# A condition layer's down products: five plain fp32 products against fifteen products of rounded pairs

## What is computed

```python
scores = softmax((x @ wt.T + repeat(g @ wg.T)) / 2)   # 8 experts, the best 2 kept, weights sum to 1
gp, up = leaky(x @ w_gate[e]), x @ w_up[e]            # 8 experts of 64 hidden columns
y = sum over the 2 chosen e of weight * (gp * up) @ w_down[e]
y = y + leaky(x @ sw_gate) * (x @ sw_up) @ sw_down    # shared expert, 128 hidden columns
```

## Time and profile before

| what | value |
|---|---|
| device time, median of 3 runs | 264.55 us (264.28 to 265.64) |
| the profiled execution's own time | 263.71 us |
| its span, first to last instruction | 261.9 us |
| TensorE busy | 246.4 us, 94% of the span |
| VectorE, ScalarE, GpSimd busy | 211.8, 147.5, 105.3 us |
| mean granted TensorE clock | 0.992 |
| share of the chain that ended last | PE 62%, DVE 17%, POOL 8%, ACT 5% |

### The profile page before, as it was taken

How to read it: one execution, slowest core, us unless ns; L and a number is a source line. 1 busy time by engine, 2 the same in 40 slices (tenths; PEclk the granted TensorE clock), 3 DMA queues, 4 the chain that set the end, 5 groups by cost and what they waited for, 6 DMA issues and landing times.

```text
span 261.9 us, 5119 instructions
## 1 busy us (share of the span) xinstructions
PE 246.4 (94%) x1848; PEld 196.8 (75%) x1848; DVE 211.8 (81%) x423; ACT 147.5 (56%) x239; POOL 105.3 (40%) x145
## 2 busy tenths in 40 slices
PE   7999999999999969988999999899999999999994
PEld 5877467667899849877687667677788888888884
DVE  7897868976876495889779987799998887888883
ACT  2666423445621454688455354687686677877550
POOL 3799310135581844864456758323220101101000
PEclk9999999999999998999999999999999999999999
DMA  6994510010210001211200000015290000000002
GB/s 169 233 271 80 210 70 0 1 43 1 30 24 0 3 5 49 71 43 43 83 4 3 6 0 0 3 58 185 96 325 26 0 0 4 0 0 0 3 1 81
DMA packets 25178, 14.54 MB, mean 56 GB/s; under 512 B 11969, under 2 KB 21862, under 8 KB 25153
## 3 DMA queue, kind: packets, MB, share of 16 engines
q1 hardware_dynamic: 24608, 13.92, 19.3%
q0 software_dynamic: 544, 0.29, 0.7%
HBM read 13.58 MB, written 0.62 MB: 54 GB/s over the span
## 4 chain that ended last, share of the span: by engine, by line
PE 62%; DVE 17%; POOL 8%; ACT 5%; issue 4%; DMA 2%; SPq 1%; DVEq 0%; ACTq 0%; POOLq 0%
PE ps L927 14%; PE ps L929 14%; PE ps L928 14%; PE ps L1086 5%; PE ps L1024 3%; POOL w_lo L503 3%; PE ps L1052 3%; PE ps L988 2%; DVE arena L1491 2%; ACT arena L747 2%; DVE arena L1699 2%; DVE arena L1681 2%; DMA w_stage<-in_L_cond_w_up 2%; DVE ssum L1672 1%; DVE arena L1643 1%
## 5 line engine op out<-in xcount | busy, mean ns | idle before, releaser
L866 ACT ACTIVATE att_bias<-ps,bias 128x512 f32<-128x512 f32 x64 | 43.5, 689 | 13.2 <-PE ps L929 13.1
L927 PE MATMUL ps<-act_hi,w_hi 128*128 128x512 f32 x120 | 48.3, 403 | 1.7 <-DVE arena L1491 0.9
L928 PE MATMUL ps<-act_lo,w_hi 128*128 128x512 f32 x120 | 47.0, 392 | 0.0
L929 PE MATMUL ps<-act_hi,w_lo 128*128 128x512 f32 x120 | 47.0, 392 | 0.0
L1771 DVE TENSOR_TENSOR g_lo<-att_bias,g_hi 128x1024 fp32r<-128x1024 f32 x32 | 39.9, 1258 | 0.6
L927 PEld LDWEIGHTS ps<-act_hi,w_hi 128*128 128x128 f32 x120 | 22.5, 188 | 8.5 <-issue 3.6
L929 PEld LDWEIGHTS ps<-act_hi,w_lo 128*128 128x128 f32 x120 | 22.5, 188 | 5.0
L928 PEld LDWEIGHTS ps<-act_lo,w_hi 128*128 128x128 f32 x120 | 22.6, 188 | 4.4
L705 ACT ACTIVATE xc<-ps 128x512 f32<-128x512 f32 x18 | 10.8, 599 | 16.0 <-PE ps L929 16.0
L1767 DVE CAST g_hi<-att_bias 128x1024 fp32r<-128x1024 f32 x16 | 12.4, 775 | 8.6 <-ACT att_bias L866 8.6
L1448 DVE TENSOR_TENSOR arena<-arena,ps 128x512 f32<-128x512 f32 x24 | 16.1, 684 | 3.4 <-PE ps L988 3.3
(11 more groups left out here) (281 smaller groups left out, 575.9 us busy)
## 6 DMA issues: line engine op xcount, KB each, us to landing
arena<-gate_m SPq DMA_DIRECT2D x16, 256.0 KB, 4.5
w_stage<-in_L_ffn_W SPq DMA_DIRECT2D x9, 256.0 KB, 2.7
w_stage<-in_L_ffn_W SPq DMA_DIRECT2D x1, 1792.0 KB, 7.8
x_tok<-in_x SPq DMA_DIRECT2D x2, 256.0 KB, 3.2
w_stage<-in_L_ffn_w_gate SPq DMA_DIRECT2D x1, 512.0 KB, 4.9
w_stage<-in_L_ffn_w_up SPq DMA_DIRECT2D x1, 512.0 KB, 6.6
w_stage<-in_L_cond_Wq SPq DMA_DIRECT2D x1, 512.0 KB, 6.4
f_down<-in_L_ffn_w_down SPq DMA_DIRECT2D x1, 512.0 KB, 6.0
```

Source lines behind the costliest of these rows:

```text
L866: act.activation(gelu[:, k % 2, b, :], bank(b), ACT.Gelu, bias=bias1[:, c:c + 1])\
L927: pe.matmul(dst, wh, xh, start=first, stop=False)
L928: pe.matmul(dst, wh, xl, start=False, stop=False)
L929: return pe.matmul(dst, wl, xh, start=False, stop=last)
```

## The change

The first half's down products stay as they are. In the second half each of the five products becomes `three(...)` of the pairs (`cd_high`, `cd_low`) for `c_down` and (`c_high`, `c_low`) for `c_hid`. The four new tiles lie in the place of `arena2`, which is written only later.

- ScalarE rounds `c_down` (128 x 640) behind the chunk of `u` = 5, and each block of `c_hid`'s second half as soon as VectorE has finished it, between the table load and `copy_hi(2)`. Chunks 14 and 15 are made behind the first two of these. The silu of the position network moves from between `copy_hi(2)` and `copy_hi(3)` to behind the tanh.
- GpSimd subtracts: `down_low` (128 x 640) and five `hidden_low` (128 x 512), all ahead of `split(12)`, and `position_rstd(0)` behind them. So `split(12)`, `split(13)` and the memset of `k_diag` come after all of that.
- TensorE waits for both semaphores ahead of each block of the second half.
- VectorE's `rp_norm(0)` moves from behind `turned(0)` to behind `turned(1)`.

```diff
+        with nc.sbuf_tensor("c_high", [P, C_BLK, HW], f32r) as c_high, \
+                nc.sbuf_tensor("c_low", [P, C_BLK, HW], f32r) as c_low, \
+                nc.sbuf_tensor("cd_high", [P, C_BLK, P], f32r) as cd_high, \
+                nc.sbuf_tensor("cd_low", [P, C_BLK, P], f32r) as cd_low:
+            pass
         arena2 = sb("arena2", [P, 8192])
...
+        SHARED_FIRST = (C_PAIRS, 0, 1, 2, 3)
...
+            def down_low():
+                pool.wait_ge(act_cdhi, 1)
+                pool.tensor_tensor(cd_low[:, :, :], c_down[:, :, :], cd_high[:, :, :].bitcast(f32), ALU.subtract).then_inc(pool_cdlo, 1)
+
+            def hidden_low(n, b):
+                pool.wait_ge(act_chi, n + 1)
+                h = c_hid[:, b, HW:TOK]
+                pool.tensor_tensor(c_low[:, b, :], h, c_high[:, b, :].bitcast(f32), ALU.subtract).then_inc(pool_clo, 1)
+
             small_tables()
             for n in range(CH_N):
+                if n == CH_Q - 2:
+                    down_low()
+                    for m, b in enumerate(SHARED_FIRST):
+                        hidden_low(m, b)
+                    position_rstd(0, 1)
                 if n == CH_Q:
-                    position_rstd(0, 1)
                     position_rstd(1, 4)
                     pool.wait_ge(v_comb, 2)
                 split(n)
...
                     chunk(next(f_chunks))
+                if u == 5:
+                    act.wait_ge(ld["cd"], 32)
+                    act.activation(cd_high[:, :, :], c_down[:, :, :], ACT.Copy).then_inc(act_cdhi, 1)
...
-            for n in f_chunks:
-                chunk(n)
             act.activation(tables[:, 2:3], eps[:, 0:1], ACT.Silu)
+
+            def hidden_high(b):
+                if b == C_PAIRS:
+                    act.wait_ge(v_hid, 2 * C_BLK)
+                else:
+                    act.wait_ge(v_mul, C_PAIRS + b + 1)
+                act.activation(c_high[:, b, :], c_hid[:, b, HW:TOK], ACT.Copy).then_inc(act_chi, 1)
+
+            for b in SHARED_FIRST:
+                hidden_high(b)
+                if b in (C_PAIRS, 0):
+                    chunk(next(f_chunks))
             copy_hi(2)
-            act.wait_ge(v_rp, 2)
-            act.activation(rp_h[:, 1, :], rp_h[:, 0, :], ACT.Silu).then_inc(act_rp, 1)
             copy_hi(3)
             act.wait_ge(pe_log, 2)
             act.activation(r_s[:, :, :], bank(4)[:, 0:P].rearrange("p (t e) -> p t e", e=F_EXP), ACT.Tanh, scale=0.5)\
                 .then_inc(act_exp, 1)
+            act.wait_ge(v_rp, 2)
+            act.activation(rp_h[:, 1, :], rp_h[:, 0, :], ACT.Silu).then_inc(act_rp, 1)
...
                 if s == 1:
                     pe.wait_ge(v_small, 4)
-                order = (C_PAIRS, 0, 1, 2, 3)
-                for n, b in enumerate(order):
+                    pe.wait_ge(pool_cdlo, 1)
+                for n, b in enumerate(SHARED_FIRST):
+                    if s == 1:
+                        pe.wait_ge(act_chi, n + 1)
+                        pe.wait_ge(pool_clo, n + 1)
+                        mm = three(bank(7), (cd_high[:, b, :], cd_low[:, b, :]), (c_high[:, b, :], c_low[:, b, :]),
+                                   first=(n == 0), last=(n == C_BLK - 1))
+                        continue
...
                 turned(s, bank(6 + s), 2)
-                if s == 0:
+                if s == 1:
                     rp_norm(0)
+                else:
                     dve.wait_ge(ld["gk"], 64)
                     link(dve.tensor_scalar(f_bias[:, :], f_bias[:, :], 0.5, None, ALU.add))
```

More of the change, by code:

```diff
@@ L281, in two_layers @@
         v_sel = sem("v_sel")
+        act_cdhi = sem("act_cdhi")
+        pool_cdlo = sem("pool_cdlo")
+        act_chi = sem("act_chi")
+        pool_clo = sem("pool_clo")
         v_warm = sem("v_warm")
@@ L1017, in _ @@
                     pe.wait_ge(v_small, 4)
-                order = (C_PAIRS, 0, 1, 2, 3)
-                for n, b in enumerate(order):
+                    pe.wait_ge(pool_cdlo, 1)
[6 more added lines that the diff above has]
+                        continue
                     if b == C_PAIRS:
-                        pe.wait_ge(v_hid, C_BLK * (s + 1))
+                        pe.wait_ge(v_hid, C_BLK)
                     else:
-                        pe.wait_ge(v_mul, C_PAIRS * s + b + 1)
-                    mm = pe.matmul(bank(6 + s), c_down[:, b, :], c_hid[:, b, s * HW:(s + 1) * HW],
+                        pe.wait_ge(v_mul, b + 1)
+                    mm = pe.matmul(bank(6), c_down[:, b, :], c_hid[:, b, 0:HW],
                                    start=(n == 0), stop=(n == C_BLK - 1))
-                    if s == 0 and n < C_PAIRS:
+                    if n < C_PAIRS:
                         spread(0, C_PAIRS + n, C_PAIRS)
```

## The result

The changed kernel took 268.22 us (median of 4 runs, 267.19 to 269.91) beside 264.56 for the kernel before (4 runs, 264.28 to 265.64): a ratio of 1.0126 [1.0086, 1.0166]. A second set of runs, beside 29 of the kernel before, gave 269.39 and 1.017 [1.0129, 1.0211]. It is slower by 1 to 2 per cent, outside the predicted range. The profiled execution took 267.19, with a span of 265.4 and a mean clock of 0.987 (before 263.71, 261.9 and 0.992).

The account below looks back on a forecast made before the run. TensorE's down products, then VectorE from `f_unit(2)`, bound the kernel. TensorE ends 0.76 earlier, but the memset's hold of `rp_norm(0)` makes `f_unit(2)` 0.3 later: 264.55 becomes 264.85 us, range 263.3 to 265.95.

Parts of the forecast that it names:

- TensorE's part: Second half's down products: ten records of 0.429 become fifteen of 0.23, 4.29 to 3.45, a gain of 0.84.
- Rival C: Second half's down products: five rests come late, TensorE waits; each 0.1 longer costs 0.5; chance 0.06 with the rest.
- ScalarE's part: Roundings around the gates and table load: load starts at 26.4, block 3 rounded at 32.8, `copy_hi(2)` not held up.
- GpSimd's durations: GpSimd's list: splits 0.70 each, `down_low` 1.55, rests 1.265 each, root 0.84, memset 1.86.
- the upper bound: `rp_norm(0)` beside the memset: L1453, ready at 38.25, waits out the memset's rest and is done at 39.7, not 38.6.
- Rival A: At `rp_norm(0)`: the memset holds nothing back, `f_unit(2)` comes 0.76 earlier, 263.8; chance 0.22.
- rival B: At the second half's L1353: memset contends with two-input subtraction, starts 0.5 later, holds L1453 to 40.15; 265.35; chance 0.12.
- The first step that failed: VectorE's L1473 at 32.19 waits 0.15 for the third rest and sets the last two rests back by 0.13.
- the rest of the first half: VectorE's L1353 at 34.41 waits until 35.0, done at 35.55; TensorE wants it at 37.75; root held back 0.5.
- where the memset meets VectorE: Memset runs from 37.8 to 39.65 and holds `rp_norm(0)`'s L1453, ready at 38.25, until its end.
- a fixed distance: Behind `f_unit(2)`: everything later follows it at the same distance as before, to the end.

Follow-up runs that it names:

- e4: Changed kernel without GpSimd's six subtractions, products reading rounded tiles instead of rests, GpSimd's list ordered as before the change; 263.9 us, ratio 0.9969.
- e5: Kernel before the change with two more memsets of `k_diag` on GpSimd behind `position_rstd(0)`; 263.72 us, ratio 0.9971.
- e7: Changed kernel with the memset at the start, `split(12)` ahead of `down_low`, `split(13)` behind the rests, root behind the first half's rest; 264.4 us, ratio 1.0001.
- e8: As e7, with VectorE's position rows also moved between the first half's copy and its rest; 264.23 us, ratio 0.9984.
- e3: Changed kernel with twelve products that nobody reads filling TensorE's wait between the router products' halves; 266.15 us, ratio 1.0049.
- e9: Changed kernel run again without edits, in the last batch; 269.39 us, ratio 1.017.
- e10: Kernel before the change with eleven products that nobody reads in TensorE's two later waits; 263.28 us, ratio 0.9946.
- e12: e3 with the later fill of e10 added; 265.13 us, ratio 1.0001.
- e1: Changed kernel with the memset of `k_diag` moved behind `position_rstd(1)`; 268.15 us, ratio 1.0143.
- e2: Changed kernel with GpSimd's splits 12 and 13 and memset held back until both halves' rests are taken; 265.14 us, ratio 1.0035.
- e6: Changed kernel with VectorE's bias addition moved behind the second half's `rp_norm(0)`; 265.83 us, ratio 1.002.

## Why the prediction was wrong

**Held up.** TensorE's part (0.84 forecast; 0.85 at `f_unit(2)` in e4). Rival C came in a small measure: the last block waited 0.14 for its rest, and the half ended 4.33 behind W where e4 has 4.08; with VectorE's copy later still, that cost nothing. ScalarE's part (table load at 25.60, last rounding in time). GpSimd's durations, the five rests ending 3.40 behind W (forecast 34.98 less 31.41, 3.57). That the memset holds a VectorE `tensor_scalar` for all of its rest, taken as the upper bound: 1.35 in the changed kernel, 0.87 and 1.62 in e5. Rival A is out by that, and rival B's mechanism too, by e5: L1355, a two-input subtraction of the very form that B names, took its 0.69 beside a running memset, and L1457 its 0.28. The Trainium skill (SBUF — State Buffer, section Who interferes with whom) states both, that a VectorE instruction in a two-port mode contends with any GpSimd instruction and that one with two SBUF inputs does not contend with one that only writes; e5 agrees, and supplied the rows that the trace of before did not have.

**The first step that failed** is L1473 (now L1515), forecast to wait 0.15 for the third rest. It waited 1.13, until the fourth had ended: GpSimd began its next subtraction ahead of the waiting VectorE. The text of rival A names this very slip and its 1.2, but made it hang on the cast, which ran in 0.14. e7 and e8 show the price in the stage: 0.57 of e7's distance is this hold.

**The second** is the rest of the first half, forecast to end at 35.55 and to cost nothing, as TensorE wants it late. It began while the root ran (34.71) and stood until both splits had ended, 1.33 too long. A rest that TensorE wants late still has the bias addition and the second half's copy queued behind it on VectorE; the prediction asked who waits for its result and not who waits for its engine.

**The third** is where the memset meets VectorE. The forecast let it start at 37.8, in front of `rp_norm(0)`. It started at 36.13 (5.54 behind W, forecast 6.39), mainly since the root was not pushed back by VectorE's rest, and met L1526, the bias addition, which stands ahead of the copy and which no step of the forecast priced. `rp_norm(0)` ran free (0.33). Together these three make 3.64, and 3.07 on the path. With the clock kept up (e3) the distance is 14.03, which is 2.26 more than before; the forecast had 0.3.

**The fourth, and the largest,** is a term that the prediction lacks: TensorE's wait of 2.85 brought the clock down to 1.2 GHz, and the next 6.5 us of work ran at that level. That is 17.02 - 14.03 = 2.99 of the 5.25. By the forecast's own times the copy was done at 36.5, before TensorE was through with the first half's eight router products (about 1.0 from 35.77). So the forecast had no wait of TensorE at that place, and it gave the clock no line. With the holds alone the kernel stands at 1.0049 (e3), about the range's upper end; the clock took it out.

**Also missed:** the later stages were taken to follow at a fixed distance. F to G did (0.04 off), but G to the end varies with the fall at 97: in the profiles it is 191.3 to 192.4 in the kernels that show none there or later (changed, e5, e9, e10, e12) and 193.0 to 194.2 in the others. Why the fall is absent in e5 and in the changed kernel, whose waits of 1.67 and 0.85 are the same as before, is open; that it is absent is shown by the windows and the mean clocks (one of the changed kernel's first four runs has 0.979, lower than the stage's fall alone gives, so it may have come there). It also comes and goes within one kernel: the profiles of e3 and e4 show it, and yet five and four of their ten runs have a mean clock of 1.000.

## What to carry to other kernels

When work is added to GpSimd, list every VectorE instruction in the stretch that GpSimd can hold (here a `tensor_scalar` from SBUF to SBUF, and beside GpSimd's subtractions also one with two SBUF inputs), and let each wait not for the running GpSimd instruction but, as an upper bound, for the whole unbroken series behind it (it waited for less in e8); then ask what is queued on VectorE behind the one that waits. When that lateness reaches TensorE, price the wait twice: its length, and, if the clock falls, the work behind it at half the clock, which here cost as much as the holds themselves (2.99 and 3.11). And look whether the kernel before has a fall of its own, since a change far ahead of it can make it come or go.

## What the runs showed of the hardware

- A VectorE instruction that stood held was passed by the next of GpSimd's back-to-back subtractions: L1515 in every kernel with the rests in that place (1.47 or 1.48 in changed, e1, e2, e3, e6, e7, e9), L1395 by two splits (2.02 or 2.03 in changed, e1, e3, e6, e9). L1515 began 0.07 ahead of the end of the third rest (31.37, 31.44) and only 0.02 ahead of the fourth's start.
- It is not passed every time. Between subtractions just as close L1518 and L1397 got in in e8 (0.62 and 1.25), and `rp_norm(0)`'s product in e2 (0.71). Between e5's two memsets L1455 did too, but those are not back to back: `link` makes GpSimd wait for the end of the first, and the second starts 0.06 behind it, where a subtraction starts 0.02 to 0.05 ahead of the end of the one before. What tells the cases apart is open.
- Not held beside a running subtraction: the cast of 63x1 (0.14), the statistics over 63x128 (0.29) and the copies out of PSUM (0.65), all in the changed kernel's VectorE timeline between 31.19 and 33.94.
- Waits of TensorE in this stage of 2.85 and 1.67 were followed by a fall of the clock, of 1.44, 1.13 and 0.34 not. The same pair of waits near 97 (1.67 and 0.85) was followed by one in the kernel before and by none in the changed kernel. So the length of one wait does not decide it alone.
